# Attention layer and feed-forward on one core: score products as pairs on 64 rows, projection tiles moved next to the value products, GpSimd additions in halves

## The chip, the core and the metric

The kernel runs on one core of a Trainium2 chip. The time is the device time of one execution in microseconds (us); lower is better. Engines are called PE (TensorE, matmuls), DVE (VectorE), ACT (ScalarE), POOL (GpSimd) and SP (SyncE, which here only issues DMAs). Each engine runs its own instruction list in order and waits for the others through semaphores.

## What is computed

One pre-norm transformer layer on `x` of shape (4, 1024, 128), 16 heads of 64:

```python
x = x + attention(layernorm(x))          # bout included
x = x + ffn(layernorm(x))                # 128 -> 32 -> 512 -> gelu -> 32 -> 128, biases b1, b2

def attention(x):
    q, k, v = x @ Wq, *split(x @ Wkv)    # heads of 64
    q, k = rope(q), rope(k)              # rotates 32 of the 64 dimensions
    sim = q @ k.T * 64 ** -0.5
    return softmax(sim) @ v @ Wout + bout
```

## The kernel before

**Groups, heads, steps.** The 64 pairs of batch and head are worked off in 16 groups of 4 heads, by a hardware loop for groups 1 to 14 and by copies of its body for the first and the last. A group has 32 steps (`STEPS`), 8 for a head; step `t` of a group makes the scores of 128 keys against all 1024 queries of head `t // 8`. "Step 14" below is the fifteenth step of a group, in head 1 of the group; its last group has no projections of a next one.

**One step.** PE makes the 128x1024 scores in one of two buffers `S` (`pe_scores`, L376 and L377), ACT takes the exponential in two halves of 512 queries into `PF`, a ring of 8 slots (L515). In even steps PE multiplies the exponentials of the two steps four and three back with V (`pe_values`, L388; the two halves of the queries go to rows 0-63 and 64-127 of `O`). POOL adds the two slots of a pair of steps into `SA` (`pool_sum`, L676), and DVE adds the four `SA` of a head into `SUM` in three instructions (`dve_sum`: part 0 in step 7 of the head, L610; parts 1 and 2 in steps 1 and 3 of the next head, L613). `SA` has two buffers, so POOL's third addition of a head waits for DVE's part 0, and so does the fourth.

**Scores in two halves of float16.** Queries and keys are each split in a high and a low float16 part. `QK` holds for each head four 128-row slots: `KHL` = high over low keys, `KMH` = a row of the constant 4096 and zeros over the high keys, `QHH` = the high queries twice, `QML` = a row of shifts over the low queries. One product KHL x QHH gives high x high + low x high; the second, KMH x QML, gives high x low and subtracts the row's estimate of its maximum. Both use all 128 rows of PE.

**The shift.** 12 steps ahead PE makes a "unit", a sample of 128 queries against all keys (`pe_unit`, L397, into the only buffer `M`), as two products of 64 rows that run side by side, and DVE takes its maximum over the keys (`dve_max`, L603). PE may not write the next unit before DVE has read the last. ACT scales the 8 maxima of a head (L501), SP moves them into the row of `QML`.

**Tiles.** Beside the scores PE makes small 128x512 "tiles" in the only buffer `TILE`; each waits until the one before has been read. They are the projections for the next group (q and k, each for two halves of the positions, as a "rot" tile that gets the rotation and a "pass" tile that doesn't; and V), the sums of exponentials over the rows ("den", L322), and the output products (L330). Tables (`QK_AT`, `V_AT`, `DEN_AT`, `OUT_AT`, ...) say in which step each is made. A rot tile goes PE, DVE (L530, L532), POOL (`rot_add`: L652, L655, one step later), ACT (`act_rot`, L451, three steps later), POOL (`rot_low`, L663, four steps later). A pass tile goes PE, ACT (L433), DVE (L535). A V tile goes PE, ACT (L441). When the last rot and pass tiles are split, SP copies them into `QK` head by head (`hand_over`, 4 DMAs each, L708 and L709); the first unit of the next group, made in step 20, needs that of head 0.

**Order within a step.** PE: in even steps values, unit, scores, tile; in odd steps scores, tile, unit. DVE: the tile of the step before, a reciprocal, `SUM`, the normalisation (`dve_norm`, L625), and last the maximum. ACT: exponentials, then the tile, then `act_rot`. POOL: `rot_low`, `rot_add`, then `pool_sum`.

Of the kernel before, what the change touches and what calls it, by code (L numbers as in the profile page):

```python
# [27 lines left out]
HAND = 4 * 16  # L28
PV_LAG = 4
# [76 lines left out]
def build(nc, x_d, wq_d, wkv_d, wout_d, bout_d, u1_d, v1_d, b1_d, u2_d, v2_d, b2_d, rope_d, ident_d, out_d):  # L106
    with ExitStack() as ctx:
# [30 lines left out]
        QK = sb("QK", [P, GH, 4, N], F16)  # L138
        KHL = QK[:, :, 0, :]
        KMH = QK[:, :, 1, :]  # L140
        QHH = QK[:, :, 2, :]
        QML = QK[:, :, 3, :]
# [3 lines left out]
        HIGH, LOW = {"k": STAGE[:, 1], "q": STAGE[:, 2]}, {"k": STAGE[:, 0], "q": STAGE[:, 3]}  # L146
# [12 lines left out]
        MX = sb("MX", [P, 2, KT], F32)  # L159
        MN = sb("MN", [P, 2, KT], F16)  # L160
# [9 lines left out]
        H = [QK[:, h, :, :].rearrange("p a b -> p (a b)").bitcast(F32) for h in range(2)]  # L170
        QT = QK[:, 3, :, :].rearrange("p a b -> p (a b)").bitcast(F32)

# [21 lines left out]
        unit_made, max_read, max_found, max_row = (sem(n) for n in ("unit_made", "max_read", "max_found", "max_row"))  # L194
# [46 lines left out]


# [150 lines left out]
        def pe_unit(e, u, place, q, bank):  # L393

            for c in range(2):
                rows, keys = slice(DH * c, DH * c + DH), slice(c * 512, (c + 1) * 512)
                mm = e.matmul(bank[:, keys], QHH[rows, place, q:N:KT], (KHL, KMH)[c][rows, place, keys],  # L397
                              start=True, stop=True)
            mm.then_inc(unit_made, 1)
# [9 lines left out]
        def pe_step(e, it, t):  # L409
            u = t + LEAD  # L410
            if t % 2 == 0:
                for back in (t - PV_LAG, t - PV_LAG + 1):
                    if back >= 0:
                        pe_values(e, it.step(back), it.i * GH + back // KT, back, it.i)
                    elif not it.first:
                        pe_values(e, it.step(back), it.i * GH - 1, back + STEPS, it.i - 1)
                if not (it.last and u >= STEPS):
                    pe_next_unit(e, it, u)
            pe_scores(e, it, t)
            pe_tiles(e, it, t)  # L420
            if t % 2 == 1 and not (it.last and u >= STEPS):
                pe_next_unit(e, it, u)


        def act_tile(e, kind, args, made, g, bank):

            if kind == "proj" and args[2] == "pass":
# [5 lines left out]
                e.activation(HIGH[w][:, 1, c * 512:(c + 1) * 512], bank, ACT.Copy).then_inc(pass_hi, 1)  # L433
# [9 lines left out]
        def act_rot(e, args, g):  # L443
# [7 lines left out]
            e.activation(HIGH[w][:, 0, c * 512:(c + 1) * 512], YR[:, :], ACT.Copy).then_inc(rot_hi, 1)  # L451
# [21 lines left out]
        def act_tiles(e, it, t):  # L473
            for n, kind, args in it.at(t):
# [7 lines left out]
                elif kind == "den":  # L482
                    act_den(e, it.pair(args), made, bank)
            for n, kind, args in it.at(t - 3):
# [12 lines left out]
        def act_max(e, head, place):  # L497

            e.wait_ge(max_read, KT * (head + 1))
            wait(e, max_row, 16 * (head - 1))  # L500
            e.activation(MN[:, place % 2, :], MX[:, place % 2, :], ACT.Copy, scale=-1.0 / MSCALE).then_inc(max_found, 1)  # L501

        def act_step(e, it, t):
# [37 lines left out]
        def dve_tiles(e, it, t):  # L541
            for n, kind, args in it.at(t - 1):
# [55 lines left out]
        def dve_max(e, u, head, place, q, bank):  # L598
# [4 lines left out]
            e.tensor_reduce(MX[:, place % 2, q:q + 1], bank, AX, ALU.max).then_inc(max_read, 1)  # L603
# [23 lines left out]
        def dve_step(e, it, t):  # L627
            u = t + LEAD
            h, kt = t // KT, t % KT
            dve_tiles(e, it, t)  # L630
# [12 lines left out]
            if not (it.last and u >= STEPS):  # L643
                dve_max(e, it.step(u), it.i * GH + u // KT, (u // KT) % GH, u % KT, M[:, :])
# [12 lines left out]
        def rot_low(e, args, g):  # L657
# [14 lines left out]
        def pool_sum(e, t, pair, free):  # L672
# [6 lines left out]
        def pool_step(e, it, t):  # L679
# [430 lines left out]
```

## Time and profile before

| | |
|---|---|
| median of 3 executions | 1556.92 us (1556.63 to 1557.19) |
| the profiled execution: its time, and its span | 1557.27 us, 1555.5 us |
| busy: PE, DVE, POOL, ACT | 1424.9, 1222.0, 977.8, 778.3 us |
| mean granted clock of PE | 0.986 of full speed |
| one group in the middle of the loop | 88.88 us |

The span runs from the first to the last instruction; the 1.8 us around it belong to the launch. Busy time of PE counts products that are in the pipeline, so neighbouring ones overlap: how long a piece of PE's work holds it is read as the distance from its start to the start of the next piece. A timeline row gives start, duration, engine, line, operation, operands and count; in brackets the idle time of the engine before it and what ended it. PEld rows are weight loads, which run beside the products.

### The profile page before, as it was taken

Reading aid. Unit: us, or ns where it says so; the run is one execution under the profiler, and the core shown is the slowest. Engines: PE = TensorE matmul, PEld = TensorE weight load, DVE = VectorE, ACT = ScalarE, POOL = GpSimd, SP = SyncE. Lnnn points to the kernel's source line nnn. Section 1 sums busy time; section 2 is a strip of 40 time slices with the busy share of each in tenths; the row PEclk is TensorE's granted clock in tenths of the full one; section 3 lists DMA queues with packets and bytes.
Section 4 is the critical chain, followed back from the end, with each engine's and each line's share of the span. In section 5 each row is a group of like instructions: output and inputs, shape, how many; then the busy total and the mean of one; then the engine's idle time right before and its main releaser. Section 6 shows DMA issues by size and latency. Waiting matters only on the chain.

```text
span 1555.5 us, 25971 instructions
## 1 busy us (share of the span) xinstructions
PE 1424.9 (92%) x7289; PEld 546.8 (35%) x7289; DVE 1222.0 (79%) x1297; ACT 778.3 (50%) x1512; POOL 977.8 (63%) x501
## 2 busy tenths in 40 slices
PE   3689999999999999999999999999999999998886
PEld 1224333333333333333333333333333333333323
DVE  7787888788788878878788888878887887888744
ACT  3244554545454545555455454545545554544464
POOL 4388766658475665838476574848566584757731
PEclk9799999999999999999999999999999999999999
DMA  5312131221303121120313122031312204031002
GB/s 158 73 26 60 25 76 26 50 54 26 83 14 75 34 57 38 44 65 14 75 34 74 22 54 54 14 79 30 75 21 54 54 20 89 14 75 33 3 15 68
DMA packets 70209, 76.00 MB, mean 49 GB/s; under 512 B 27204, under 2 KB 36936, under 8 KB 69928
## 3 DMA queue, kind: packets, MB, share of 16 engines
q1 hardware_dynamic: 68736, 74.69, 21.4%
q10 hardware_dynamic: 1448, 1.00, 0.3%
q8 instruction: 13, 0.21, 0.1%
q14 instruction: 12, 0.10, 0.0%
HBM read 22.56 MB, written 2.36 MB: 16 GB/s over the span
## 4 chain that ended last, share of the span: by engine, by line
PE 56%; DVE 13%; issue 13%; POOL 7%; DMA 5%; ACT 3%; SPq 2%; DVEq 0%; ACTq 0%; POOLq 0%
PE O L388 18%; PE S L376 10%; PE S L377 8%; PE M L397 8%; DVE MX L603 5%; PE TILE L312 5%; DVE SUM L613 4%; DMA QK<-STAGE 4%; POOL SA L676 3%; PE TILE L322 2%; POOL STAGE L663 2%; ACT PF L515 2%; SPq L708 1%; PE TILE L306 1%; PE TILE L330 1%
## 5 line engine op out<-in xcount | busy, mean ns | idle before, releaser
L676 POOL TENSOR_TENSOR SA<-PF 128x1024 f32<-128x1024 f32 x256 | 616.5, 2424 | 372.5 <-DVE SUM L610 279.9
L515 ACT ACTIVATE PF<-S 128x512 f32<-128x512 f32 x1024 | 547.8, 599 | 564.9 <-PE S L377 564.1
L603 DVE TENSOR_REDUCE MX<-M 128x1 f32<-128x1024 f32 x504 | 614.5, 1219 | 229.3 <-PE M L397 229.1
L388 PE MATMUL O<-PF,V 128*64 128x512 f32 x2048 | 497.4, 607 | 0.0
L376 PE MATMUL S<-QK 128*128 128x512 f16 x1024 | 393.1, 384 | 0.0
L377 PE MATMUL S<-QK 128*128 128x512 f16 x1024 | 390.1, 381 | 0.0
L397 PE MATMUL M<-QK 64*128 64x512 f16 x1008 | 221.9, 437 | 65.9 <-DVE MX L603 47.7
L613 DVE TENSOR_TENSOR SUM<-SUM,SA 128x1024 f32<-128x1024 f32 x128 | 248.3, 1939 | 3.6 <-POOL SA L676 3.4
L397 PEld LDWEIGHTS M<-QK 64*128 64x128 f16 x1008 | 72.6, 140 | 370.8 <-DVE MX L603 247.9
L388 PEld LDWEIGHTS O<-PF,V 128*64 128x64 f32 x2048 | 124.5, 136 | 206.4 <-issue 149.8
L376 PEld LDWEIGHTS S<-QK 128*128 128x128 f16 x1024 | 99.9, 98 | 165.3 <-issue 64.2
L652 POOL TENSOR_TENSOR T<-T,ROPE 128x512 f32<-128x512 f32 x60 | 76.3, 1271 | 127.8 <-DVE T L532 127.8
L494 ACT ACTIVATE OS<-O 64x512 f32<-64x512 f32 x128 | 75.8, 592 | 130.8 <-PE O L388 130.0
L377 PEld LDWEIGHTS S<-QK 128*128 128x128 f16 x1024 | 100.7, 98 | 76.8 <-issue 1.4
L655 POOL TENSOR_TENSOR YR<-T 128x512 f32<-128x512 f32 x60 | 113.1, 1886 | 4.7
L663 POOL TENSOR_TENSOR STAGE<-YR,STAGE 128x512 f16<-128x512 f32 x64 | 97.7, 1526 | 21.1 <-ACT STAGE L451 21.1
L312 PE MATMUL TILE<-XT,WQK 128*128 (+1 forms) x372 | 102.4, 385 | 6.3 <-ACT V L441 2.6
L610 DVE TENSOR_TENSOR SUM<-SA 128x1024 f32<-128x1024 f32 x64 | 81.8, 1278 | 19.8 <-ACT DS L471 19.8
L330 PE MATMUL TILE<-WO,OS 128*128 (+1 forms) x504 | 68.9, 280 | 16.9 <-DVE OS L625 14.7
L625 DVE TENSOR_TENSOR OS<-OS,RB 128x1024 f32<-128x1024 f32 x32 | 78.7, 2460 | 6.4 <-DMA RB<-den 6.4
L330 PEld LDWEIGHTS TILE<-WO,OS 128*128 128x128 f32 x504 | 65.6, 194 | 31.5 <-issue 21.7
L539 DVE TENSOR_TENSOR X<-TILE,X 128x512 f32 (+1 forms) x63 | 43.2, 685 | 29.4 <-PE TILE L330 29.4
(96 smaller groups left out, 749.0 us busy)
## 6 DMA issues: line engine op xcount, KB each, us to landing
QK<-STAGE SPq DMA_DIRECT2D x128, 256.0 KB, 3.9
QK<-STAGE SPq DMA_DIRECT2D x128, 128.0 KB, 3.1
RB<-den SPq DMA_DIRECT2D x128, 128.0 KB, 3.0
X<-in_L_attn_queries SPq DMA_DIRECT2D x4, 512.0 KB, 12.8
RT<-DS SPq DMA_DIRECT2D x128, 2.0 KB, 1.7
out<-X SPq DMA_DIRECT2D x8, 256.0 KB, 2.3
WRAW<-in_L_attn_Wkv SPq DMA_DIRECT2D x1, 1024.0 KB, 8.7
ROPE<-in_rope SPq DMA_DIRECT2D x1, 1024.0 KB, 12.0
```

Source lines behind the costliest of these rows:

```text
L312: mm = e.matmul(bank, WQK[:, "qk".index(w), wp, kind, cols], XT[:, xp, rows], start=(n == 0), stop=(n == 2))
L330: mm = e.matmul(bank[:, j * P:(j + 1) * P], OS[:, parity, z, j * P:(j + 1) * P], WO[:, pair, :], start=True, stop=True)
L376: e.matmul(S[:, t % 2, rows], KHL[:, h, keys], QHH[:, h, rows], start=True, stop=False)
L377: e.matmul(S[:, t % 2, rows], KMH[:, h, keys], QML[:, h, rows], start=False, stop=True).then_inc(scored, 1)
L388: mm = e.matmul(O[DH * z:DH * z + DH, :], V[:, h, kt * DH:(kt + 1) * DH], PF[:, t % SLOTS, z * HALF:(z + 1) * HALF], start=(kt == 0), stop ...
L397: mm = e.matmul(bank[:, keys], QHH[rows, place, q:N:KT], (KHL, KMH)[c][rows, place, keys], start=True, stop=True)
L515: e.activation(PF[:, t % SLOTS, z * HALF:(z + 1) * HALF], S[:, t % 2, z * HALF:(z + 1) * HALF], ACT.Exp, scale=EXP_SCALE).then_inc(exped, 1)
L603: e.tensor_reduce(MX[:, place % 2, q:q + 1], bank, AX, ALU.max).then_inc(max_read, 1)
L613: e.tensor_tensor(SUM[:, h % 2, :], SUM[:, h % 2, :], SA[:, part - 1, :], ALU.add).then_inc(summed, 1)
L655: e.tensor_tensor(YR[:, :], T1[:, :], T2[:, :], ALU.add).then_inc(rot_sum, 1)
L663: e.tensor_tensor(LOW[w][:, 0, cols], YR[:, :], HIGH[w][:, 0, cols], ALU.subtract).then_inc(rot_lo, 1)
L676: e.tensor_tensor(SA[:, (t // 2) % 2, :], PF[:, t % SLOTS, :], PF[:, t % SLOTS + 1, :], ALU.add).then_inc(two_summed, 1)
```

## The change

1. **Scores.** `QK` has three slots for each head. The queries' first half and a copy of the keys stand on rows 0-63, the second half and another copy on rows 64-127. A step makes four pairs of 64-row products (high x high, high x low, low x high, constant x shift), one of a pair on each half of the rows, for one half of the queries each. The constant and the shifts get tensors of their own, `MSC` and `MQ`. The last pair alone waits for the shift.
2. **Units** keep two 64-row products, now one for each half of the queries; the maximum is 128x2, and DVE merges the two halves once for each head (`dve_merge`). SP sends the shifts in two DMAs.
3. **Order on PE.** Even steps: values, tile, unit, scores. Odd steps: scores, unit, tile. So a tile stands right behind or right ahead of the value products. On ACT the tile of an even step comes ahead of the exponentials, and `act_rot` stays last. On DVE the maximum is first in a step, and the tile is worked off in its own step.
4. **POOL** adds in two instructions of 512 columns, and `pool_sum` is first in a step, ahead of `rot_low` and `rot_add`.
5. **Tables.** q and k tiles in steps 0, 2, 4, 7, 9, 11, 13, 15; V tiles in 17, 18, 24, 26 (before 8, 10, 22, 24); den in 6 and 22; output tiles in 19, 21, 29, 31; `dve_norm` in 15 and 27; SP sends the shifts of head 3 ahead of the sums.

```diff
+ROWS = 2 * 16
-QK_AT = (1, 3, 5, 7, 9, 11, 13, 15)
-V_AT = {8: (1, 0), 10: (1, 1), 22: (0, 0), 24: (0, 1)}
-DEN_AT = {6: 1, 20: 0}
+QK_AT = (0, 2, 4, 7, 9, 11, 13, 15)
+V_AT = {17: (1, 0), 18: (1, 1), 24: (0, 0), 26: (0, 1)}
+DEN_AT = {6: 1, 22: 0}
-NORM_AT = {16: 1, 26: 0}
-OUT_AT = {17: (1, 0), 19: (1, 1), 28: (0, 0), 30: (0, 1)}
+NORM_AT = {15: 1, 27: 0}
+OUT_AT = {19: (1, 0), 21: (1, 1), 29: (0, 0), 31: (0, 1)}
...
         def pe_scores(e, it, t):
+            for z in range(2):
+                wait(e, exped, 2 * n + z - 3)
+                e.matmul(S[:, t % 2, z * HALF:(z + 1) * HALF], KH[z][:, h, keys], QH[z][:, h, :],
+                         start=True, stop=False)
+            for z in range(2):
+                e.matmul(S[:, t % 2, z * HALF:(z + 1) * HALF], KH[z][:, h, keys], QL[z][:, h, :],
+                         start=False, stop=False)
+            for z in range(2):
+                e.matmul(S[:, t % 2, z * HALF:(z + 1) * HALF], KL[z][:, h, keys], QH[z][:, h, :],
+                         start=False, stop=False)
             if kt == 0:
-                e.wait_ge(max_row, 16 * (it.i * GH + h + 1))
+                e.wait_ge(max_row, ROWS * (it.i * GH + h + 1))
             for z in range(2):
-                rows = slice(z * HALF, (z + 1) * HALF)
-                wait(e, exped, 2 * n + z - 3)
-                e.matmul(S[:, t % 2, rows], KHL[:, h, keys], QHH[:, h, rows], start=True, stop=False)
-                e.matmul(S[:, t % 2, rows], KMH[:, h, keys], QML[:, h, rows],
+                side = slice(DH * z, DH * z + DH)
+                e.matmul(S[:, t % 2, z * HALF:(z + 1) * HALF], MSC[side, :], MQ[side, h, :],
                          start=False, stop=True).then_inc(scored, 1)
...
         def pe_step(e, it, t):
+                pe_tiles(e, it, t)
                 if not (it.last and u >= STEPS):
                     pe_next_unit(e, it, u)
-            pe_scores(e, it, t)
-            pe_tiles(e, it, t)
-            if t % 2 == 1 and not (it.last and u >= STEPS):
-                pe_next_unit(e, it, u)
+                pe_scores(e, it, t)
+            else:
+                pe_scores(e, it, t)
+                if not (it.last and u >= STEPS):
+                    pe_next_unit(e, it, u)
+                pe_tiles(e, it, t)
...
+        def dve_merge(e, head, place):
+
+            e.wait_ge(max_read, KT * (head + 1))
+            e.tensor_tensor(MX[:, place % 2, :, :], MXP[:, place % 2, 0, :, :], MXP[:, place % 2, 1, :, :],
+                            ALU.max).then_inc(max_merged, 1)
...
-            e.tensor_tensor(SA[:, (t // 2) % 2, :], PF[:, t % SLOTS, :], PF[:, t % SLOTS + 1, :],
-                            ALU.add).then_inc(two_summed, 1)
+            for z in range(2):
+                part = slice(z * HALF, (z + 1) * HALF)
+                add = e.tensor_tensor(SA[:, (t // 2) % 2, part], PF[:, t % SLOTS, part], PF[:, t % SLOTS + 1, part],
+                                      ALU.add)
+            add.then_inc(two_summed, 1)
```

**Order on POOL, steps 13 to 16.** `SA<-PF` is `pool_sum`, `T<-T,ROPE` and `YR<-T` are `rot_add` of the rot tile of step 13, `STAGE<-YR,STAGE` is `rot_low`. Before:

```order
L663 TENSOR_TENSOR STAGE<-YR,STAGE 128x512 [waits rot_hi]
L651 REGISTER_ALU
L652 TENSOR_TENSOR T<-T,ROPE 128x512 [waits rot_read]
L655 TENSOR_TENSOR YR<-T 128x512 [waits rot_lo,rot_parts]
L674 ISA
L212 REGISTER_ALU [waits exped]
L676 TENSOR_TENSOR SA<-PF 128x1024 [waits summed]
```

Now:

```order
L701 TENSOR_TENSOR STAGE<-YR,STAGE 128x512 [waits rot_hi]
L712 ISA
L217 REGISTER_ALU [waits exped]
L716 TENSOR_TENSOR SA<-PF 128x512 [waits summed]
L716 TENSOR_TENSOR SA<-PF 128x512
L690 REGISTER_ALU
L691 TENSOR_TENSOR T<-T,ROPE 128x512 [waits rot_read]
L694 TENSOR_TENSOR YR<-T 128x512 [waits rot_lo,rot_parts]
```

The rotation of that tile moved behind the addition of the exponentials of steps 12 and 13, the one that waits for DVE's part 0 of the same head (`summed`).

**Order on DVE, steps 15 and 16.** `MX<-M` (now `MXP<-M`) are the maxima, `SUM<-SA` is part 0, `STAGE<-TILE,STAGE` the pass tile of step 15, `OS<-OS,RB` the normalisation. Before:

```order
L610 TENSOR_TENSOR SUM<-SA 128x1024 [waits den_copied]
L600 REGISTER_ALU
L603 TENSOR_REDUCE MX<-M 128x1 [waits unit_made]
L534 REGISTER_ALU
L535 TENSOR_TENSOR STAGE<-TILE,STAGE 128x512 [waits pass_hi]
L624 ISA [waits spread_in]
L625 TENSOR_TENSOR OS<-OS,RB 128x1024 [waits o_copied]
```

Now:

```order
L633 TENSOR_REDUCE MXP<-M 128x2 [waits unit_made]
L564 REGISTER_ALU
L565 TENSOR_TENSOR STAGE<-TILE,STAGE 128x512 [waits pass_hi]
L644 ISA
L217 REGISTER_ALU [waits two_summed]
L647 TENSOR_TENSOR SUM<-SA 128x1024 [waits den_copied]
L661 ISA [waits spread_in]
L662 TENSOR_TENSOR OS<-OS,RB 128x1024 [waits o_copied]
```

Part 0 moved from the front of step 15 behind the maximum of that step and behind the pass tile made in it.

**Order on ACT, steps 16 and 17.** `STAGE<-YR` is `act_rot` of the rot tile of step 13, `PF<-S` are exponentials. Before, the rows behind it are the exponentials of step 17 and the copy of `O`:

```order
L451 ACTIVATE STAGE<-YR 128x512 [waits rot_sum]
L511 ISA
L515 ACTIVATE PF<-S 128x512 [waits two_summed,pv_done,scored]
L511 REGISTER_ALU
L515 ACTIVATE PF<-S 128x512 [waits scored]
L494 ACTIVATE OS<-O 64x512 [waits added,pv_done]
```

Now:

```order
L474 ACTIVATE STAGE<-YR 128x512 [waits rot_sum]
L539 ISA
L543 ACTIVATE PF<-S 128x512 [waits two_summed,pv_done,scored]
L539 REGISTER_ALU
L543 ACTIVATE PF<-S 128x512 [waits scored]
L459 REGISTER_ALU
L464 ACTIVATE V<-TILE 128x4x2x64 [waits pv_done,tile_made]
```

Behind the exponentials of step 17 now comes the copy of the V tile of that step, for which PE's V tile of step 18 waits.

## Rows read from the trace of the kernel before

**Rows 1.** Busy time by engine in one group of the loop (us, instructions):

```profile
690.00:778.88 88.88, 84.92 (x440) 32.41 (x438) 71.92 (x68) 45.26 (x90) 57.20 (x28) 1.00 0.22 48
```

**Rows 2.** Timeline of PE, steps 14 to 20 of that group:

```profile
731.22 0.44 PE L397 MATMUL M<-QK 64*128 64x512 f16 x2
731.59 0.39 PE L376 MATMUL S<-QK 128*128 128x512 f16 x1
...
733.32 0.81 PE L312 MATMUL TILE<-XT,WQK 128*128 x3
734.07 0.44 PE L397 MATMUL M<-QK 64*128 64x512 f16 x2
734.43 1.94 PE L388 MATMUL O<-PF,V 128*64 128x512 f32 x8
736.30 0.44 PE L397 MATMUL M<-QK 64*128 64x512 f16 x2
...
743.37 0.44 PE L397 MATMUL M<-QK 64*128 64x512 f16 x2 [0.78 <-DVE MX L603]
...
749.27 0.44 PE L397 MATMUL M<-QK 64*128 64x512 f16 x2 [0.51 <-DMA QK<-STAGE]
```

**Rows 3.** Who waited for whom: total us, times, longest:

```profile
POOL SA L676 <- DVE SUM L610: 279.9, 48, 8.9
...
PE M L397 <- DVE MX L603: 47.7, 56, 2.8
...
PE M L397 <- DMA QK<-STAGE: 17.0, 16, 6.5
...
PE TILE L330 <- DVE OS L625: 14.7, 15, 5.8
```

**Rows 4.** Timeline of PE and its weight loads, the first units, half clock:

```profile
41.76 0.65 PE L397 MATMUL M<-QK 64*128 64x512 f16 x2 [6.51 <-DMA QK<-STAGE]
41.77 0.19 PEld L397 LDWEIGHTS S<-QK 64*128 64x128 f16 x2
42.18 1.09 PE L397 MATMUL S<-QK 64*128 64x512 f16 x4
```

**Rows 5.** Timeline of DVE, POOL and ACT, steps 15 to 18:

```profile
732.95 1.40 DVE L610 TENSOR_TENSOR SUM<-SA 128x1024 f32<-128x1024 f32 x1
733.35 2.13 POOL L655 TENSOR_TENSOR YR<-T 128x512 f32<-128x512 f32 x1
...
735.45 5.65 POOL L676 TENSOR_TENSOR SA<-PF 128x1024 f32<-128x1024 f32 x2
735.68 0.68 DVE L535 TENSOR_TENSOR STAGE<-TILE,STAGE 128x512 f16<-128x512 f32 x1
736.28 2.59 DVE L625 TENSOR_TENSOR OS<-OS,RB 128x1024 f32<-128x1024 f32 x1
...
737.40 1.08 ACT L515 ACTIVATE PF<-S 128x512 f32<-128x512 f32 x2 [2.54 <-PE S L377]
738.37 0.63 ACT L451 ACTIVATE STAGE<-YR 128x512 f16<-128x512 f32 x1
...
741.05 2.13 POOL L663 TENSOR_TENSOR STAGE<-YR,STAGE 128x512 f16<-128x512 f32 x1
742.10 1.21 DVE L603 TENSOR_REDUCE MX<-M 128x1 f32<-128x1024 f32 x1
...
743.85 1.23 DVE L603 TENSOR_REDUCE MX<-M 128x1 f32<-128x1024 f32 x1
...
744.99 1.59 DVE L613 TENSOR_TENSOR SUM<-SUM,SA 128x1024 f32<-128x1024 f32 x1
```

**Rows 6.** Page, costliest groups: busy us, mean ns, idle before:

```profile
L613 DVE TENSOR_TENSOR SUM<-SUM,SA 128x1024 f32<-128x1024 f32 x128 | 248.3, 1939 | 3.6 <-POOL SA L676 3.4
...
L652 POOL TENSOR_TENSOR T<-T,ROPE 128x512 f32<-128x512 f32 x60 | 76.3, 1271 | 127.8 <-DVE T L532 127.8
...
L610 DVE TENSOR_TENSOR SUM<-SA 128x1024 f32<-128x1024 f32 x64 | 81.8, 1278 | 19.8 <-ACT DS L471 19.8
```

More of the change, by code:

```diff
@@ L393, in pe_unit @@
         def pe_unit(e, u, place, q, bank):
[L395 to L398, printed above, removed]
+            part, half = q // 2, q % 2
+            for z in range(2):
+                mm = e.matmul(bank[:, z * HALF:(z + 1) * HALF], QH[z][:, place, part:HALF:KT // 2],
+                              KH[z][:, place, half * 512:(half + 1) * 512], start=True, stop=True)
             mm.then_inc(unit_made, 1)
@@ L629, in dve_step @@
             h, kt = t // KT, t % KT
+            if not (it.last and u >= STEPS):
+                dve_max(e, it.step(u), it.i * GH + u // KT, (u // KT) % GH, u % KT, M[:, :])
+            if u % KT == 0 and not (it.last and u > STEPS):
+                dve_merge(e, it.i * GH + u // KT - 1, (u // KT - 1) % GH)
             dve_tiles(e, it, t)
@@ L675, in pool_sum @@
             wait(e, summed, free)
-            e.tensor_tensor(SA[:, (t // 2) % 2, :], PF[:, t % SLOTS, :], PF[:, t % SLOTS + 1, :],
-                            ALU.add).then_inc(two_summed, 1)
+            for z in range(2):
+                part = slice(z * HALF, (z + 1) * HALF)
+                add = e.tensor_tensor(SA[:, (t // 2) % 2, part], PF[:, t % SLOTS, part], PF[:, t % SLOTS + 1, part],
+                                      ALU.add)
+            add.then_inc(two_summed, 1)
         def pool_step(e, it, t):
+            if t % 2 == 0 and (not it.first or t > 0):
+                back = t - 2
+                head, part = it.i * GH + back // KT, (back % KT) // 2
+                pool_sum(e, back % STEPS, it.i * (STEPS // 2) + back // 2, 3 * head + (-1, 0, 1, 1)[part])
             for n, kind, args in it.at(t - 4):
@@ L685, in pool_step @@
                     rot_add(e, args, it.i + 1)
-            if t % 2 == 0 and (not it.first or t > 0):
-                back = t - 2
-                head, part = it.i * GH + back // KT, (back % KT) // 2
-                pool_sum(e, back % STEPS, it.i * (STEPS // 2) + back // 2, 3 * head + (-1, 0, 1, 1)[part])
             if it.first and t - 2 in STATS_AT:
@@ L714, in max_over @@
             wait(sp, scored, head * 16 - 48)
-            row = QML[0:1, place, :].rearrange("o (p t) -> o p t", t=KT)
-            sp.dma_start(row, MN[:, place % 2, :]).then_inc(max_row, 16)
+            for z in range(2):
+                row = MQ[DH * z:DH * z + 1, place, :].rearrange("o (p t) -> o p t", t=KT // 2)
+                sp.dma_start(row, MN[:, place % 2, z, :]).then_inc(max_row, 16)
         def den_over(sp, what, q):
@@ L797, in _ @@
             pool.wait_ge(powers_set, 1)
-            for n, (rows, side, value) in enumerate(((DH, 1, 0.0), (1, 1, MSCALE), (DH, 3, 0.0))):
-                pool.memset(QK[0:rows, :, side, :], value).then_inc(set_up, 1)
-                pool.wait_ge(set_up, n + 1)
+            pool.memset(MQ[:, :, :], 0.0).then_inc(set_up, 1)
+            pool.memset(MSC[:, :], 0.0).then_inc(set_up, 1)
+            pool.wait_ge(set_up, 2)
+            for z in range(2):
+                pool.memset(MSC[DH * z:DH * z + 1, :], MSCALE).then_inc(set_up, 1)
+                pool.wait_ge(set_up, 3 + z)
             pool.memset(ONES[:, :], 1.0).then_inc(set_up, 1)
-            pool.wait_ge(set_up, 4)
+            pool.wait_ge(set_up, 5)
             ln_rstd(pool, 0)
```

78 lines of the change are left out of this document (46 added, 32 removed).

## The prediction

> **What bounds the kernel now.** I read the busy time of one group first. PE is busy 84.9 of 88.88 us, DVE 71.9, POOL 57.2, ACT 45.3 [rows 1], so PE sets the pace and DVE is the only other engine that is nearly full. Then PE's timeline, from start to start [rows 2]. A unit holds PE 0.37 us ahead of scores (731.22 to 731.59), though its side-by-side products stream 512 columns, which take 0.216 at full clock (eight score products take 1.73). So 0.16 is lost when PE goes from 64-row products to full ones. A projection tile, three such streams or 0.65, takes 0.75 ahead of a unit (733.32 to 734.07): 0.10 lost from full to 64-row. A unit ahead of the values takes 0.36, 0.15 lost; the values take 1.87 (734.43 to 736.30) for four passes of 0.427, 0.16 lost. These losses come at every change of shape, and the change of order and rows is about them. Last, the real waits of PE for others: (47.7 + 14.7 + 17.0 - 6.5) / 16 = 4.6 us in a group [rows 3]; the 6.5 is ahead of the loop.
>
> **What the new order takes away.** Before, a pair of steps has four changes of shape: values, unit, scores, unit, values. With two more for each den tile a group has 16 x 4 + 2 x 2 = 68, worth 16 x (0.16 + 0.16 + 0.10 + 0.15) + 0.5 = 9.6 us. Now scores and units have one shape, so a pair has two changes, and each of the 18 tiles, which stands at an end of the values, adds one: 50. With 0.16 for each one out of the 64-row or value shape and 0.10 into it from a full tile, that is 32 x 0.16 + 18 x 0.10 = 6.9. The step from values to a full tile is in no row; I take 0.16 of the nearest (unit to scores), the bounds are 0.10 and 0.16. Gain: 2.7 us in a group, at most 3.2.
>
> **What the four pairs cost.** The score products stream 4 pairs x 0.216 = 0.86 us in a step, as the four full ones did, if each pair runs side by side and its weights load behind the pair before. At full clock no row has two pairs in a row. At half clock one does: the second unit starts 0.42 after the first, one stream of 512 columns at 1.2 GHz, and its two weight loads started at 41.77, while the first unit ran on the same rows [rows 4]. So I cost it at nothing.
>
> The Trainium skill says otherwise: in "TensorE: Matmul & The Clock Gate", Part 3, The mechanism, a weight load overlaps running products only where the row group differs. By it each pair would add its load to the stream. The row at 41.77 speaks against that, so it is a rival with a small chance, below.
>
> **POOL in halves.** DVE and POOL block each other for whole instructions when DVE's operands both lie in SBUF. Two additions of POOL took 5.65 us, with the normalisation between them, and that took 2.59; the tile subtraction at 735.68, with one operand in PSUM, took its 0.68 [rows 5]. A `SUM` part costs 1.2 free and 1.94 on average for parts 1 and 2 [rows 6]. Halves of 1.27 (the 512-column row of [rows 6]) halve what DVE waits: some 0.4 x 8 + 0.6 x 2 = 4 us of DVE in a group, which counts only where DVE is late. POOL pays 2 x 1.27 instead of 2.33, hidden in its idle 31 us unless POOL is in the chain. The merge, at most 0.2 four times, and the second DMA of the shifts have several us of cover.
>
> **Where DVE is late now.** A reduction starts 0.48 after its unit (743.37, 743.85), the next DVE operation 1.14 later (744.99), and the next unit may start 1.27 after it (742.10 to 743.37) [rows 2, 5]. So units can follow at 1.75. From the unit of an even step to that of the odd one PE now has 0.22 + 1.73 = 1.95 (before 2.20 or more): DVE's lateness in an even step is paid in full beyond 0.2. Counting from an even unit, DVE is free at 1.95 + 0.48 + 1.14 = 3.57 and the next even unit wants it at 0.48 + 1.95 + 0.37 + 1.87 = 4.67, or 5.4 with one tile.
> - Steps 26/27: part 2 and normalisation, 3.57 + 1.2 + 1.2 = 6.0, up to 7.2 with a wait for POOL, against 4.67. I take 1.8 us of wait; 1.1 to 2.3.
> - Steps 8/9: rot tile 1.2, reciprocal 0.2, part 1 1.2 to 2.4, against 5.4: POOL is just then in its fourth addition, so I take 1.2; 0.5 to 1.6.
> - Steps 6/7 and 10/11: the pass tile waits for ACT until 4.05 (derived below), then 0.7 + 1.2: 0.7 together; 0.3 to 1.4.
>
> With 0.1 elsewhere that is 3.8 in the group outside steps 14 to 20; before it was 4.6 less 2.3 (1.0, 0.78 and 0.51 [rows 2, 3]) = 2.3. So +1.5, between -0.4 and +3.
>
> **Steps 14 to 20.** Here the order on POOL bites. Before, unit 14 to unit 20 takes 749.27 - 731.22 = 18.05 us, and the rotation of tile 13 is over at 733.35 + 2.13 = 735.48, ahead of the two additions that waited for part 0 [rows 2, 5]. They do so in 48 heads of 64, 279.9 us in all [rows 3]; in the 16 others the rotation fills that time. Now it stands behind the first of them. With unit 14 at 0:
> - Scores end 1.95. ACT began 0.73 after the scores (736.67 would be 736.30 + 0.37, to 737.40 [rows 2, 5]), of which 0.43 is the first half; both halves now end with the step, so exponentials of step 14 start at 0.22 + 0.87 + 0.30 = 1.4 and those of 15 end at 3.4. ACT copies tile 15 until 4.0.
> - DVE: reduction 15 until 3.57, wait, tile subtraction from 4.05 to 4.7, part 0 to 5.9, normalisation to 7.1. POOL gets its go at 5.9, but the normalisation is under way.
> - POOL: addition 7.1 to 9.6; first half of the rotation to 10.9; part 1 of step 17 on DVE slips in, to 12.0; second half to 13.3.
> - ACT, in order: `act_rot` to 13.9, exponentials of step 17 to 14.9, copy of V tile 17 to 15.5. PE's V tile 18 waits for that, from 11.4 to 15.6. (Unit 17 has waited 1.5 for reduction 16.) Unit 18: 16.3.
> - POOL: fourth addition to 15.8, `rot_low` to 17.0. From its end to unit 20 it took 749.27 - 743.18 = 6.1 before (hand-over DMAs [rows 2, 5]): unit 20 at 23.1; PE alone would be there at 21.5.
>
> So this stretch gets 5.0 us longer. With neither collision on the port (5.9 as the start of the addition, no part 1 in between) the chain is 2.6 shorter, 20.5, or +2.4; with one more collision of 1.2, +6.2.
>
> **Sum.** Without waits the stretch is as long as before to 0.2 (four tiles instead of three), so the 2.7 lies in the rest. A group: -2.7 + 1.5 + 5.0 = +3.8; I take 3.4, since I chose the collisions' high side in two of four places. Fifteen groups prepare a next one: +51. The last has no projection or hand-over and gains some 2. Profiled 1557.3 + 49 = 1606; its median lies 0.35 lower, which I neglect. Bounds: low 15 x (-2.7 + 2.4 - 0.4) - 2 = -13, or 1544; high 15 x (-2.7 + 6.2 + 3) - 2 = +96, or 1653.
>
> **Rivals.**
> - *The shape changes win (faster).* If DVE and POOL don't meet and part 0 comes before the normalisation blocks POOL, the time is between 1544 and, with no more wait than before, 1557 - 16 x 2.7 = 1514. For: DVE has 17 us idle in a group and the halves free 4 more. Against: the order of four queues, which no luck on the port changes. It decides at 20.8 us for the stretch with the rest as before (18.05 + 2.7). 0.24.
> - *Both cancel*: the same balance within 0.2 us a group, 1554 to 1560. 0.06.
> - *Weights of 64-row pairs are not hidden*: + 0.19 (a load in [rows 4]) x 4 x 512 = 389 us, 1946; or pairs don't run side by side, + 0.86 x 512 = 440, about 2000. Against: [rows 4]. 0.03.
> - *More lateness than I found*, 1628 to 1660, since a delayed step also delays POOL's next addition. 0.09.
> - *Forecast*, 1560 to 1628, 1606 likeliest: 0.58.
>
> **How the numbers follow.** Slower by over 0.2%, about what a measurement of this kernel can tell: 0.58 + 0.09 + 0.03 = 0.70; faster 0.24; same 0.06. The range leaves out half of the fast rival and all beyond 1628: 1535 to 1628.
>
> **What will show it.** Right: from scores to unit PE takes no 0.16 and units of one pair of steps are 1.95 apart; V tile 18 waits several us for ACT's copy of tile 17; ACT waits for POOL's rotation in step 16; POOL idles ahead of its third addition in head 1 while the rotation is queued; a group is near 92 us. Wrong: if the additions in step 14 start before 6, or if `act_rot` finds its tile done, the forecast falls to the fast rival; if pairs of score products are over 0.25 apart, to the slow one.

## The result: 4.2% slower

| | median | lowest to highest |
|---|---|---|
| before | 1557.06 us | 1556.63 to 1559.14 (4 executions) |
| changed | 1623.41 us | 1620.08 to 1625.15 (4 executions) |

The ratio is 1.042, with a 95% interval of 1.040 to 1.044. The forecast was 1606 us, range 1535 to 1628, with 0.70 for slower.

First the changed kernel's page: granted clock of PE in 40 slices, then groups as in [rows 6] and, behind them, lines of who waited for whom as in [rows 3].

```profile
L716 POOL TENSOR_TENSOR SA<-PF 128x512 f32<-128x512 f32 x512 | 697.3, 1388 | 490.5 <-DVE SUM L647 393.9
...
L474 ACT ACTIVATE STAGE<-YR 128x512 f16<-128x512 f32 x64 | 41.2, 644 | 91.7 <-POOL YR L694 87.3
```

```profile
POOL SA L716 <- DVE SUM L647: 393.9, 63, 10.6
...
ACT STAGE L474 <- POOL YR L694: 87.3, 30, 5.8
...
PE TILE L317 <- ACT V L464: 51.4, 15, 4.0
```

The mean granted clock is 0.963 of full speed (before 0.986). POOL waited for part 0 in 48 heads before and in 63 now: the 15 more are the ones in which the rotation of tile 13 used to end after part 0. The later part 0 makes them wait, not the place of the rotation: with the rotations ahead again (the first experiment) it is 63 as well. In the 15 groups that prepare a next one PE's V tile waits for ACT, and ACT waits for POOL's rotation in 30 places. None of these two lines was there before.

This is the timeline of PE, DVE, POOL and ACT from unit 14 (758.00) to unit 20 (780.72) of a group, the stretch of [rows 2, 5]:

```profile
758.00 0.41 PE L417 MATMUL M<-QK 64*128 64x512 f16 x2
...
762.58 1.22 DVE L647 TENSOR_TENSOR SUM<-SA 128x1024 f32<-128x1024 f32 x1
762.90 0.41 PE L417 MATMUL M<-QK 64*128 64x512 f16 x2
...
763.71 1.22 DVE L662 TENSOR_TENSOR OS<-OS,RB 128x1024 f32<-128x1024 f32 x1
...
763.87 3.40 POOL L716 TENSOR_TENSOR SA<-PF 128x512 f32<-128x512 f32 x2 [5.32 <-DVE SUM L647]
...
766.12 0.41 PE L417 MATMUL M<-QK 64*128 64x512 f16 x2 [1.08 <-DVE MXP L633]
766.46 1.24 PE L317 MATMUL TILE<-WV,XT 128*128 x12
...
767.24 1.26 POOL L691 TENSOR_TENSOR T<-T,ROPE 128x512 f32<-128x512 f32 x1
...
767.71 1.87 DVE L650 TENSOR_TENSOR SUM<-SUM,SA 128x1024 f32<-128x1024 f32 x1
768.58 2.12 POOL L694 TENSOR_TENSOR YR<-T 128x512 f32<-128x512 f32 x1
...
770.73 0.63 ACT L474 ACTIVATE STAGE<-YR 128x512 f16<-128x512 f32 x1 [5.35 <-POOL YR L694]
...
772.22 0.60 ACT L464 ACTIVATE V<-TILE 128x512 f32<-128x512 f32 x1
...
772.96 1.36 PE L317 MATMUL TILE<-WV,XT 128*128 x12 [3.39 <-ACT V L464]
...
780.72 0.41 PE L417 MATMUL M<-QK 64*128 64x512 f16 x2
```

Read it from below. V tile 18 (772.96) has waited 3.39 us for ACT's copy of V tile 17 (772.22). ACT stood for 5.35 us ahead of the rotated tile 13 (770.73), whose last instruction on POOL ended at 770.70. POOL had been idle for 5.32 us until part 0 ended, with the rotation queued behind the addition, and then stood behind the normalisation: its two halves took 3.40 us, not 2.48. Part 1 slipped in between the two instructions of the rotation, as in the forecast. The stretch takes 22.72 us against 18.05. Over the 14 groups of the loop the mean is 23.02 against 18.09.

### The profile page after: what moved, and what is told of

It reads as the page before. It is cut to its first block, busy times and chain, and to the rows that moved or that the text cites. A ratio compares the mean times of both kernels' runs of the same rounds, so it can differ in the third digit from the quotient of the medians.

```text
span 1623.3 us, 30516 instructions
## 1 busy us (share of the span) xinstructions
PE 1426.9 (88%) x9337; PEld 543.5 (33%) x9337; DVE 1200.1 (74%) x1361; ACT 788.8 (49%) x1512; POOL 1034.1 (64%) x758
## 4 chain that ended last, share of the span: by engine, by line
PE 35%; POOL 24%; issue 23%; DVE 9%; DMA 3%; ACT 3%; SPq 2%; DVEq 0%; POOLq 0%; ACTq 0%
POOL SA L716 13%; PE O L408 11%; PE TILE L341 4%; PE M L417 4%; DVE MXP L633 4%; POOL STAGE L701 3%; POOL YR L694 3%; PE S L385 3%; PE S L388 3%; PE S L397 3%; PE S L391 3%; POOL T L691 2%; PE TILE L317 2%; DMA RT<-DS 2%; SPq L766 2%
## 5 line engine op out<-in xcount | busy, mean ns | idle before, releaser
L716 POOL TENSOR_TENSOR SA<-PF 128x512 f32<-128x512 f32 x512 | 697.3, 1388 | 490.5 <-DVE SUM L647 393.9
L633 DVE TENSOR_REDUCE MXP<-M 128x2 f32<-128x1024 f32 x504 | 615.9, 1222 | 319.8 <-PE M L417 319.2
L417 PE MATMUL M<-QK 64*128 64x512 f16 x1008 | 206.7, 406 | 83.5 <-DVE MXP L633 71.8
L650 DVE TENSOR_TENSOR SUM<-SUM,SA 128x1024 f32<-128x1024 f32 x128 | 230.5, 1800 | 4.3 <-POOL SA L716 4.3
L385 PE MATMUL S<-QK 64*128 64x512 f16 x1024 | 202.4, 390 | 0.0
L388 PE MATMUL S<-QK 64*128 64x512 f16 x1024 | 201.6, 389 | 0.0
L391 PE MATMUL S<-QK 64*128 64x512 f16 x1024 | 200.9, 388 | 0.0
L397 PE MATMUL S<-MQ,MSC 64*128 64x512 f16 x1024 | 200.0, 386 | 0.0
L417 PEld LDWEIGHTS M<-QK 64*128 64x128 f16 x1008 | 57.4, 110 | 307.5 <-DVE MXP L633 156.9
L317 PE MATMUL TILE<-WV,XT 128*128 (+1 forms) x756 | 67.0, 238 | 51.9 <-ACT V L464 51.4
L474 ACT ACTIVATE STAGE<-YR 128x512 f16<-128x512 f32 x64 | 41.2, 644 | 91.7 <-POOL YR L694 87.3
L317 PEld LDWEIGHTS TILE<-WV,XT 128*128 (+1 forms) x756 | 51.9, 104 | 98.1 <-issue 87.9
```

What stands on the lines that cost most here:

```text
L317: mm = e.matmul(bank[:, r * P:(r + 1) * P], XT[:, xp, rows], WV[:, wp, cols], start=(n == 0), stop=(n == 2))
L385: e.matmul(S[:, t % 2, z * HALF:(z + 1) * HALF], KH[z][:, h, keys], QH[z][:, h, :], start=True, stop=False)
L388: e.matmul(S[:, t % 2, z * HALF:(z + 1) * HALF], KH[z][:, h, keys], QL[z][:, h, :], start=False, stop=False)
L391: e.matmul(S[:, t % 2, z * HALF:(z + 1) * HALF], KL[z][:, h, keys], QH[z][:, h, :], start=False, stop=False)
L397: e.matmul(S[:, t % 2, z * HALF:(z + 1) * HALF], MSC[side, :], MQ[side, h, :], start=False, stop=True).then_inc(scored, 1)
L417: mm = e.matmul(bank[:, z * HALF:(z + 1) * HALF], QH[z][:, place, part:HALF:KT // 2], KH[z][:, place, half * 512:(half + 1) * 512], start= ...
```

## The group of 88.88 us was a misreading

The document ahead of the prediction gives 88.88 us for a group. That window starts at the unit of one group and ends at no matching place of the next. PE's timeline of before has the values of step 0 of two groups in a row:

```profile
689.94 1.94 PE L388 MATMUL O<-PF,V 128*64 128x512 f32 x8
```

```profile
779.48 1.94 PE L388 MATMUL O<-PF,V 128*64 128x512 f32 x8
```

A group took 89.5 us. In the changed kernel it is 93.2, from tile 0 to tile 0:

```profile
720.18 0.82 PE L323 MATMUL TILE<-XT,WQK 128*128 x3
```

```profile
813.40 0.82 PE L323 MATMUL TILE<-XT,WQK 128*128 x3
```

From one unit 20 to the next the mean over the loop is 89.56 us before and 93.47 now. The forecast is a sum of differences, so the 88.88 doesn't enter it; the group it ends in, "near 92", was low by some 0.6 us for this reason, the rest comes below.

## The experiments

Theory A is the forecast's: DVE does part 0 late, POOL's addition waits for it, and the rotation, ACT and PE's V tile queue up behind. Theory B: the 64-row pairs, the halves or the moved tiles are slower in themselves, and the wait just shows up there. All times are medians of four executions or more, each beside the kernel before at 1556.6 to 1556.9 us.

### Rotations ahead of the addition again

```diff
         def pool_step(e, it, t):
-            if t % 2 == 0 and (not it.first or t > 0):
-                ... pool_sum(...)
             for n, kind, args in it.at(t - 4):
                 ... rot_low(e, args, it.i + 1)
             for n, kind, args in it.at(t - 1):
                 ... rot_add(e, args, it.i + 1)
+            if t % 2 == 0 and (not it.first or t > 0):
+                ... pool_sum(...)
```

> The changed kernel with one thing back: on POOL rot_low and rot_add stand ahead of pool_sum again, in every step. Theory A (queue order): in the changed kernel the rotation of tile 13 waits behind the addition that waits for part 0 (770.70 instead of about 760), ACT waits 5.35 us for it, V tile 18 waits 3.39 us for ACT, and PE's clock falls after that. With the rotation ahead V tile 18 starts without a wait, ACT's wait is gone, the granted clock goes back from 0.963 to about 0.985. Unit 14 to unit 20 then ends with the hand-over: fourth addition to 11.9, rot_low to 13.1, DMAs 6.4, so 19.5 instead of 22.7 us; a group loses 3.2 us, 15 groups 48: about 1575 us. Theory B (the 64-row pairs, the halves or DVE's new order make the kernel slower, and the rotation's place is incidental): the wait moves to the next place and the time stays above 1610.

Measured: 1570.24 us, ratio 1.009 (1.007 to 1.010). 53 of the 66 us are gone with the place of the three small instructions that POOL runs for a rotation, in all steps. The timeline of POOL, ACT and PE in the same stretch (unit 14 is at 733.12):

```profile
736.15 1.27 POOL L694 TENSOR_TENSOR YR<-T 128x512 f32<-128x512 f32 x1
...
740.39 0.63 ACT L474 ACTIVATE STAGE<-YR 128x512 f16<-128x512 f32 x1
...
745.79 1.16 POOL L701 TENSOR_TENSOR STAGE<-YR,STAGE 128x512 f16<-128x512 f32 x1
...
753.08 0.41 PE L417 MATMUL M<-QK 64*128 64x512 f16 x2 [2.37 <-DMA QK<-STAGE]
```

POOL rotates at 736, in the time in which it is idle for part 0 anyway, ACT doesn't wait, and neither does the V tile. What is late next is the hand-over: `rot_low` still stands behind both additions, and unit 20 waits 2.37 us for the DMAs. 19.96 us for the stretch were measured, 19.5 expected.

### Only the rotation of tile 13

```diff
+            for n, kind, args in it.at(t - 1) if t == 14 else ():
+                ... rot_add(e, args, it.i + 1)
             if t % 2 == 0 and (not it.first or t > 0):
                 ... pool_sum(...)
...
-            for n, kind, args in it.at(t - 1):
+            for n, kind, args in it.at(t - 1) if t != 14 else ():
                 ... rot_add(e, args, it.i + 1)
```

> The changed kernel with rot_add ahead of pool_sum in step 14 alone (the rotation of tile 13); everywhere else pool_sum stays first. Theory A says that step 14 is the place: within 8 us of the run with all of them back, about 1575. If the order in the other steps matters (rot_low in steps 4, 8, 17, rot_add in step 10), this run stays nearer to 1600. Theory B: above 1610.

Measured: 1600.80 us, ratio 1.028. This missed: 23 us of the 53, though the V tile's wait is gone and ACT's is down from 87.3 us to 6.5. Theory A is right in the mechanism and too narrow in the place. A group takes 92.0 us in the mean over the loop, against 90.1 with all rotations first. Some 1 us of the difference lies in steps 5 to 13, most of it where unit 13 waits for a late reduction (0.68; none with all rotations first). The other 0.9 us lies behind unit 20, in PE's clock, below. The order on POOL costs in two places.

### Part 0 a step earlier

```diff
-SUM_AT = {7: 0, 1: 1, 3: 2}
+SUM_AT = {6: 0, 1: 1, 3: 2}
```

> The changed kernel with DVE's part 0 one step earlier: in step 6 of each head, not in step 7. POOL's order stays as changed, the rotation behind the addition. Theory A says that the rotation's place only hurts because that addition waits for a late part 0. Part 0 then ends 2.8 us after unit 14 and not 5.9, the addition runs to 5.3, the rotation to 7.8, ACT waits 0.5 and not 5.35 us, V tile 18 doesn't wait, unit 20 comes at 17.9 (hand-over) and not 22.7: with some of the waits around steps 6 to 11 gone, 5.7 us a group, 1535 to 1545 us. Theory B (the place of the rotation itself costs, whatever part 0 does): near the second experiment, 1600.

Measured: 1542.91 us, ratio 0.991 (0.989 to 0.992), as expected. The steps on the way are less well met: ACT still waits 1.58 us for the rotation and not 0.5, and unit 20 comes 19.6 us after unit 14 and not 17.9. POOL's order is that of the changed kernel, and the loss is gone all the same, with more than the first experiment gave. So most of what the rotation's place costs it costs behind an addition that waits. With the run before, this shows both links of the chain: take either away and V tile 18 no longer stands. The gain of 80 us is not all from this chain, since part 0 moved in every head: units 9 and 13 no longer wait, and units 11, 17 and 29 wait less. ACT's wait, which V tile 18 hardly feels:

```profile
731.34 0.63 ACT L474 ACTIVATE STAGE<-YR 128x512 f16<-128x512 f32 x1 [1.58 <-POOL YR L694]
```

### The shape of the scores alone

The kernel before with the pairs, the layout, the merge and the two DMAs; order, tables and POOL as before.

```diff
-                e.matmul(S[:, t % 2, rows], KHL[:, h, keys], QHH[:, h, rows], start=True, stop=False)
-                e.matmul(S[:, t % 2, rows], KMH[:, h, keys], QML[:, h, rows],
-                         start=False, stop=True).then_inc(scored, 1)
+                e.matmul(S[:, t % 2, z * HALF:(z + 1) * HALF], KH[z][:, h, keys], QH[z][:, h, :],
+                         start=True, stop=False)
...
+                e.matmul(S[:, t % 2, z * HALF:(z + 1) * HALF], MSC[side, :], MQ[side, h, :],
+                         start=False, stop=True).then_inc(scored, 1)
```

> The kernel before with the 64-row pairs, the new layout, the merge and the two DMAs alone; order, tables and POOL's additions as before. By the count of shape changes: values-unit 0.16 and unit-values 0.15 in 16 pairs, and 18 tiles amid 64-row work at 0.26 each, together 9.7 us a group, as before (9.6). So no gain without the move of the tiles: 1550 to 1570. If the pairs by themselves cost (weights not hidden, both halves of the scores ready only at the end): 1580 or more; if they gain by themselves: under 1540.

Measured: 1558.85 us, ratio 1.002 (1.001 to 1.003). In the old order the pairs cost 2 us and gain nothing, as the count of shape changes had it. Theory B's first part falls, and so does the rival of the weights that are not hidden.

### The halves on the kernel before and on the changed one

```diff
-            e.tensor_tensor(SA[:, (t // 2) % 2, :], PF[:, t % SLOTS, :], PF[:, t % SLOTS + 1, :],
-                            ALU.add).then_inc(two_summed, 1)
+            for z in range(2):
+                part = slice(z * HALF, (z + 1) * HALF)
+                add = e.tensor_tensor(SA[:, (t // 2) % 2, part], PF[:, t % SLOTS, part], PF[:, t % SLOTS + 1, part],
+                                      ALU.add)
+            add.then_inc(two_summed, 1)
```

> The kernel before with POOL's addition in two instructions of 512 columns, nothing else. Theory: DVE's SUM parts 1 and 2 fall from 1.94 to about 1.6 us and the normalisation from 2.46 to under 2.0; of PE's 4.5 us of waits in a group some 1 to 1.5 go (step 2, steps 16 to 18, step 26): 1533 to 1542. Rival: PE's waits don't hang on the length of POOL's instruction, POOL only gets busier: 1555 to 1560.

Measured: 1540.86 us, ratio 0.991 (0.989 to 0.993): the halves alone make the kernel before faster by 16 us. PE's waits for reductions fell from the 47.7 us of [rows 3] to 22.9 us; the hand-over took some of it back, 35.4 instead of 17.0:

```profile
PE M L397 <- DMA QK<-STAGE: 35.4, 16, 6.5
PE M L397 <- DVE MX L603: 22.9, 42, 2.8
```

The reverse edit on the changed kernel:

> The changed kernel with POOL's addition in one instruction of 1024 columns again. Theory A: the halves help, since DVE waits at most 1.24 us instead of 2.33 for an addition under way; the mean of SUM parts 1 and 2 goes from 1.80 to over 2.0 us, the waits behind steps 8/9, 10/11 and 26/27 grow by 1 to 2 us a group: 1638 to 1655. Rival (the halves are part of the loss, since POOL's additions take 2.48 instead of 2.33 for a pair and POOL is in the chain of steps 14 to 18, two additions): a group gains 0.3 to 0.5 us, 1616 to 1619.

Measured: 1629.37 us, ratio 1.046, 6 us more than the changed kernel. The sign was right, the size not (1638 to 1655 were expected): SUM parts 1 and 2 went from 1.80 to 1.85 us, not over 2.0, and PE's waits for reductions from 71.8 to 74.7 us. That the chain of four queues hides DVE's waits here is my reading; no run shows it by itself.

### DVE's work in even steps

```diff
         (rotations ahead of pool_sum, as in the first experiment)
-SUM_AT = {7: 0, 1: 1, 3: 2}
+SUM_AT = {6: 0, 0: 1, 2: 2}
-NORM_AT = {15: 1, 27: 0}
+NORM_AT = {16: 1, 26: 0}
-DEN_AT = {6: 1, 22: 0}
+DEN_AT = {6: 1, 20: 0}
```

> The changed kernel with POOL's old order (rotations ahead of pool_sum), DVE's SUM parts in steps 6, 0 and 2 of a head (before 7, 1, 3), the normalisations in steps 16 and 26, den in 6 and 20. From the timeline: between the reductions of an even and an odd step DVE has 0.8 us free, and behind an even step's work the odd unit has a slack of 1.1 us or more, so work belongs in even steps. Theory A: the waits of the first experiment at units 17 (1.24), 9 and 11 (1.2), 27 to 29 (1.9) and at the hand-over (2.37) go; a group falls from 89.4 to 83 to 85 us: 1480 to 1510, which would beat both kernels. Rival: DVE or POOL is full by then and the waits only move: 1540 or more.

Measured: 1500.70 us, ratio 0.964 (0.962 to 0.965). With another order on POOL and other steps for DVE's work, the change is worth 3.6%; the order of two queues hid that. Which share DVE's new steps would have brought to the kernel before was not tried. A group takes 85.4 us. What is left is in steps 16 and 26, each with a SUM part and a normalisation ahead of the next reduction; here is unit 18 of PE and the DVE work ahead of it:

```profile
710.26 2.07 DVE L650 TENSOR_TENSOR SUM<-SUM,SA 128x1024 f32<-128x1024 f32 x1
...
712.25 2.29 DVE L662 TENSOR_TENSOR OS<-OS,RB 128x1024 f32<-128x1024 f32 x1
...
714.47 1.21 DVE L633 TENSOR_REDUCE MXP<-M 128x2 f32<-128x1024 f32 x1
...
715.74 0.41 PE L417 MATMUL M<-QK 64*128 64x512 f16 x2 [1.23 <-DVE MXP L633]
```

### The normalisations in steps 17 and 27

```diff
-NORM_AT = {16: 1, 26: 0}
+NORM_AT = {17: 1, 27: 0}
```

> The kernel with DVE's work in even steps, with the normalisations in steps 17 and 27 in place of 16 and 26. In that kernel step 16 holds part 1 and a normalisation ahead of reduction 17, and unit 18 waits 1.23 us for it; step 26 holds part 2 and a normalisation, and unit 28 waits 0.92. Theory A (what counts is the sum of DVE's work between two reductions against the time to the next unit: 0.8 us in an even step plus what the odd step's window leaves): one in each step takes both waits away, 1.8 to 2.2 us a group, 1468 to 1476. Rival: step 17's normalisation meets POOL's two additions or POOL's rot_low of tile 13, the hand-over gets later and unit 20 waits instead: 1490 to 1505.

Measured: 1493.49 us, ratio 0.959 (0.958 to 0.961), the fastest kernel here. It lies in the rival's range (1490 to 1505), above theory A's 1468 to 1476. The wait at unit 18 went, but unit 20 then waited 0.9 us for the hand-over, as the rival said, and the wait of step 26 only moved to unit 29 (0.78 us):

```profile
PE M L417 <- DVE MXP L633: 28.3, 58, 1.4
PE M L417 <- DMA QK<-STAGE: 21.3, 16, 6.6
```

### Full-row scores in the new order

The run with DVE's work in even steps, with scores and units as in the kernel before; the layout of `QK`, the maxima and the DMAs for them go back too (the lines shown leave that out and shorten the calls):

```diff
-            for z in range(2):
-                e.matmul(..., KH[z][:, h, keys], QH[z][:, h, :], ...)      # and three pairs more
+            for z in range(2):
+                e.matmul(S[:, t % 2, rows], KHL[:, h, keys], QHH[:, h, rows], start=True, stop=False)
+                e.matmul(S[:, t % 2, rows], KMH[:, h, keys], QML[:, h, rows], start=False, stop=True)
```

> The same order, tables and halves as in the run with DVE's work in even steps, but scores and units as in the kernel before: two products on 128 rows for each half of the queries, 128x1 maxima, no merge. It prices the change of shape alone: units next to scores cost 0.16 going in and 0.10 coming out, 16 pairs x 0.26 x 16 groups = 66 us more than with 64-row pairs, less what the later exponentials cost there. Expected 55 to 70 us above that run. Rival: if shape changes are cheap and pairs cost as much as they save, within 15 us of it.

Measured: 1540.67 us, 40 us above that run; 55 to 70 were expected. PE's timelines tell why. Full rows first, then pairs: the unit of an even step, its scores, and the unit of the odd one.

```profile
721.56 0.44 PE L397 MATMUL M<-QK 64*128 64x512 f16 x2
721.93 0.39 PE L376 MATMUL S<-QK 128*128 128x512 f16 x1
...
723.76 0.43 PE L397 MATMUL M<-QK 64*128 64x512 f16 x2
724.13 0.39 PE L312 MATMUL TILE<-XT,WQK 128*128 x1
```

```profile
727.21 0.41 PE L417 MATMUL M<-QK 64*128 64x512 f16 x2
727.45 0.38 PE L385 MATMUL S<-QK 64*128 64x512 f16 x2
727.67 0.38 PE L388 MATMUL S<-QK 64*128 64x512 f16 x2
...
729.18 0.38 PE L417 MATMUL M<-QK 64*128 64x512 f16 x2
729.49 0.65 PE L408 MATMUL O<-PF,V 128*64 128x512 f32 x2
```

The sequence takes 2.57 us with full rows and 2.28 with pairs (what follows the odd unit, a tile or the values, differs, but not what is counted up to its start). That is 0.29 a pair of steps, and 16 x 16 x 0.29 = 74 us by estimate, even more than the 66. But with a shorter sequence DVE has less time between units: PE's waits for reductions are 27.4 us with full rows and 48.1 with pairs. DVE takes 21 of the 74 back; where the other 13 went was not followed up.

This run is also as fast as the halves alone on the kernel before (1540.86). So the new order, the tables and DVE's new steps bring nothing on top of the halves as long as the scores keep full rows, and the pairs bring nothing in the old order. It takes both, and the halves too, as the next run shows.

### Whole additions in the good order

> The kernel with DVE's work in even steps and POOL's old order, with POOL's addition in one instruction of 1024 columns. On the kernel before the halves gave 16 us, on the changed kernel only 6. Theory: they are worth what DVE's waiting costs PE. Here SUM parts follow a reduction at once, in a step with 0.8 us to spare, so a wait of up to 2.33 instead of 1.24 us for POOL is paid: 1510 to 1525. Rival: with the parts placed early the halves no longer matter: 1498 to 1504.

The edit is the one that puts POOL's addition back in one instruction. Measured: 1549.87 us, 49 us more than with halves, where 10 to 25 were expected. The mean of SUM parts 1 and 2 is 1.95 us instead of 1.56. The page, and the timeline of DVE and POOL ahead of unit 18:

```profile
L650 DVE TENSOR_TENSOR SUM<-SUM,SA 128x1024 f32<-128x1024 f32 x128 | 249.9, 1952 | 3.5 <-POOL SA L714 3.3
```

```profile
730.99 2.36 POOL L714 TENSOR_TENSOR SA<-PF 128x1024 f32<-128x1024 f32 x1
...
731.39 3.04 DVE L650 TENSOR_TENSOR SUM<-SUM,SA 128x1024 f32<-128x1024 f32 x1
...
737.72 0.46 PE L417 MATMUL M<-QK 64*128 64x512 f16 x2 [1.94 <-DVE MXP L633]
```

Part 1 was issued 0.4 us after an addition had begun, stood for the rest of it, about 1.9 us, and that wait reached PE. PE's waits for reductions are 92.0 us in this run, 48.1 with halves, which is 44 of the 49. The same edit was worth 6, 16 and 49 us in three orders.

The Trainium skill, "SBUF — State Buffer", section "SBUF: two separate sides", has the rule: the port pair that DVE and GpSimd share is an exclusive lock, kept for the whole instruction by whoever comes first. These rows agree: part 1 took 3.04 us, 1.96 of them until the addition's end.

## Point by point: the forecast's steps

Slower was right, and by the chain that was forecast. The size is 66 us where 49 were forecast, 5 us inside the upper end of the range. In the profiled runs, the forecast's base, it is 68 us: 59 up to the last hand-over and 9 from there to the end.

- **Shape changes, 2.7 us a group**: right in total, wrong in parts. From values to a full tile 0.16 was taken and is measured (1.87 from values to tile). Scores and units have nothing between them, as assumed. The change from 64 rows to full or values, taken at 0.15 to 0.16, costs 0.10 when a unit follows scores (729.18 to 729.49 less 0.216), so there was a bit more to gain. Outside the stretch a group went from 89.6 - 18.1 = 71.5 to 93.5 - 23.0 = 70.5, by -1.0; the forecast had -2.7 + 1.5 = -1.2.
- **Four pairs at nothing**: right. Pairs start 0.216 apart at full clock (727.45, 727.67). The Trainium skill's rule ("TensorE: Matmul & The Clock Gate", Part 3, The mechanism), by which weights of the same row group would not load behind a running pair, doesn't hold in these rows: successive pairs use the same two row groups. The same section also names a background weight buffer, for which weights may be loaded early; that would fit these rows.
- **DVE late in steps 26/27, 8/9, 6/7 and 10/11, 3.8 us**: 4.3 measured. Unit 29 waited 1.43 in brackets and 1.6 by its distance, 1.8 forecast; unit 11 1.2 (1.2); units 9 and 13 1.0 together (0.7); 0.3 at unit 25 and 0.2 at den 6 (0.1). The work in question is that of steps 27, 9, 7 and 11, and the unit that waits for it is the one two steps later.
- **POOL in halves, 4 us of DVE's waits in a group**: the total is near (parts 1 and 2 from 1.94 to 1.80 us, the normalisation from 2.46 to 1.28, together 3.5 us a group), the cause mostly another. With whole additions on the changed kernel the normalisation takes 1.29 too, so its new place did that; the halves are worth 0.05 us on each of the eight parts, 0.4 us a group.
- **Steps 14 to 20, +5.0**: +4.7 in the group shown, +4.9 in the mean. Counted from unit 14: part 0 to 5.8 (5.9), addition over at 9.3 (9.6), rotation over at 12.7 (13.3), V tile 18 at 15.0 (15.6), unit 20 at 22.7 (23.1). Of the collisions on the port, both that were forecast took place. The last link was luck: the forecast had the hand-over end the stretch, with PE ready 1.6 us earlier. In 13 of 15 groups unit 20 doesn't wait for the hand-over, because PE, at half clock behind the V tile's wait, gets there no earlier. The forecast had no term for the clock. In the one loop group whose clock stayed up (below), unit 20 waited and the stretch took 22.40 us, +4.3. (The lower bound has an error too: without the two collisions its chain is 1.2 + 1.1 = 2.3 shorter by its own figures, not 2.6, which puts that bound at 1549.)
- **The term that was mis-sized** is the rounding behind the sum: "+3.8; I take 3.4, since I chose the collisions' high side in two of four places". Both took place, and the mean is +3.9 over the loop (89.56 to 93.47). 15 x 3.9 = 58, not 51. There was no reason in a row for the discount: in all 15 groups V tile 18 waited for ACT, 3.37 to 4.00 us, so the queues left little to chance.
- **The last group, -2**: also wrong, and by more. From the unit 20 that waits for the last hand-over to the end it was 9 us longer (188.4 against 179.2 us). I had not worked out that group. With the rotations first it is 187.1, with part 0 a step earlier 182.0, with DVE's work in even steps 179.5. So DVE's late work, part 0 above all, makes up most of it, and the order on POOL little; which wait carries it was not followed up.
- **The rivals**: the fast one was the right mechanism for the wrong kernel. With the order of queues repaired the time is 1501, under its 1514. Its price of 16 x 2.7 is borne out in total by the first point; what it missed is that the waits of before could go as well.

## To carry to other kernels

When a cheap edit reorders an in-order queue, ask of each instruction that now stands ahead what it waits for, and who waits behind it on the other engines: here three instructions of 1.2 to 1.3 us moved behind one that waited, and cost 53 us over four queues; two of them, in one step, cost 23. Work off the chain by hand from rows; it came out within 0.7 us in 22, collisions included, so don't discount it afterwards. And try each part of a mixed change alone: the halves gained 16 us by themselves, the pairs nothing by themselves and 40 us in the right order, and the order of two queues lost it all.

## What the runs showed of the hardware

**The clock follows a wait, but not each.** Windows of the changed kernel: us, busy time of PE, PEld, DVE, ACT and POOL, then the granted clock of PE, the share of the DMA engines, GB/s.

```profile
766.12:772.96 6.84, 3.45 (x22) 1.51 (x23) 3.01 (x2) 2.21 (x5) 6.76 (x5) 1.00 0.00 0
772.96:774.20 1.24, 1.24 (x12) 0.96 (x12) 0.00 (x0) 1.07 (x2) 1.24 (x2) 0.67 0.00 0
774.20:776.70 2.50, 2.50 (x14) 0.89 (x14) 1.23 (x1) 0.61 (x2) 2.50 (x3) 0.50 0.39 75
776.70:780.72 4.02, 4.02 (x27) 1.77 (x24) 2.80 (x3) 2.06 (x4) 0.00 (x0) 0.99 0.96 196
```

Through the wait of 3.39 us the clock stays at 1.00, and right after it, with PE busy again, it is at 0.50, that is 1.2 GHz, for over 2.5 us. The eight pairs of steps 18 and 19 take 2.79 us here and 2.22 to 3.41 in other groups, instead of 1.73. In one group of 15 they take 1.73, after the same wait:

```profile
959.17 1.13 PE L317 MATMUL TILE<-WV,XT 128*128 x12 [3.39 <-ACT V L464]
960.23 0.41 PE L417 MATMUL M<-QK 64*128 64x512 f16 x2
...
966.60 0.41 PE L417 MATMUL M<-QK 64*128 64x512 f16 x2 [1.07 <-DMA QK<-STAGE]
```

There unit 20 waited 1.07 us for the hand-over instead, so PE would have waited anyway: the stretch takes 22.40 us in this group and 23.02 in the mean, and the drop is worth some 0.6 us a group. After waits of 2.4 us for the hand-over the eight pairs of steps 20 and 21 took 1.73 us in 8 of the loop's 14 groups in the first experiment, and in 1 of 14 in the second (3.1 to 3.3 us in most others), though the mean waits are equal to 0.02 us. With part 0 a step earlier it was 4 of 14, after waits of 2.1 us. What tells them apart stays open; no run here varied it by itself.

**Tiles of short products are slower close behind a unit.** The V tile of twelve 128-column products takes 0.78 us when PE comes to it from the values, and 1.17 in step 17 of the changed kernel, behind unit 17, for which PE has just waited 1.08 us, at full clock in both cases. The wait isn't the whole of it. With DVE's work in even steps unit 17 doesn't wait, and the tile takes 0.97 us, from its start to that of the values:

```profile
710.82 1.04 PE L317 MATMUL TILE<-WV,XT 128*128 x12
711.79 1.94 PE L408 MATMUL O<-PF,V 128*64 128x512 f32 x8
```

In the same place with full-row scores and no wait it takes 0.77. PE's sequencer has register instructions between these products. That their issue sets the pace when PE arrives early is an argument, not shown.
